# Routed rows that hold their last 64 features twice, so that one product turns two groups of 128 rows

## The reference

```
pooled = x.reshape(64, 12, 14, 16, 14, 16).sum(axis=(3, 5))
h = einsum('bcij,ce->bije', pooled, channel_weights).reshape(64, 196, 192)
h = h + attention(layernorm(h))        # 12 heads, weights relu(1 + qk + qk^2/2), normalised
flat = layernorm(h)                    # 12544 tokens of 192 features
top_w, top_i = top_k(softmax(flat @ router_w.T), 2)   # 2 of 8 experts
out = h + sum over the 2 experts of w_e * (gelu(flat @ w1[e] + b1[e]) @ w2[e] + b2[e])
```

## Time and profile before

| | us |
|---|---|
| median of 3 runs | 1308.08 (1303.27 to 1308.3) |
| profiled execution, its own time | 1309.67 |
| its span, first to last instruction | 1307.8 |
| TensorE busy | 1207.0 (92%) |
| VectorE busy | 883.9 (68%) |
| ScalarE busy | 593.6 (45%) |
| GpSimd busy | 559.2 (43%) |

### The profile page before, as it was taken

One profiled execution on the slowest core, in us unless ns is written; L12 is line 12 of the kernel. 1 busy time (PEld: TensorE's weight loads), 2 busy tenths in 40 slices (PEclk: granted clock), 3 DMA queues, 4 the chain that ended last, 5 costly groups with the idle time before them and its releaser, 6 DMA issues.

```text
span 1307.8 us, 25915 instructions
## 1 busy us (share of the span) xinstructions
PE 1207.0 (92%) x7219; PEld 1078.2 (82%) x7219; DVE 883.9 (68%) x2860; ACT 593.6 (45%) x1143; POOL 559.2 (43%) x453
## 2 busy tenths in 40 slices
PE   5867865999999999999999999999999899999996
PEld 3756754888889788989898989898989788899996
DVE  6788887686969686878778787878755332233443
ACT  0222223453545454545454545454545544545564
POOL 0103332315445445453636363635463654443533
PEclk9986556999999999999999999999999999999998
DMA  9789987778888788879798978798744655444555
GB/s 354 232 283 346 347 317 248 208 231 237 240 256 236 236 234 250 226 241 255 237 257 236 256 240 251 238 255 251 184 125 81 200 131 107 100 108 90 119 140 116
DMA packets 124823, 284.41 MB, mean 217 GB/s; under 512 B 23091, under 2 KB 68772, under 8 KB 124772
## 3 DMA queue, kind: packets, MB, share of 16 engines
q1 hardware_dynamic: 82570, 241.95, 55.8%
q0 software_dynamic: 41568, 41.24, 18.7%
q10 hardware_dynamic: 634, 0.61, 0.2%
HBM read 228.79 MB, written 54.95 MB: 217 GB/s over the span
## 4 chain that ended last, share of the span: by engine, by line
PE 68%; DVE 15%; issue 7%; ACT 4%; another core or an unknown queue 2%; DMA 2%; SPq 1%; ACTq 0%; DVEq 0%; POOLq 0%; POOL 0%
PE ps L1005 24%; PE ps L974 20%; PE ps L814 6%; PE ps L921 3%; PE ps L910 3%; DVE red L1086 2%; PE ps L945 2%; PE ps L946 2%; PE ps L888 2%; PE ps L900 2%; DVE red L1083 1%; PE ps L878 1%; DVE topi L1222 1%; DVE w1l L1342 1%
## 5 line engine op out<-in xcount | busy, mean ns | idle before, releaser
L631 POOL DMA_INDIRECT result<-ys,ridx x210 | 333.6, 1589 | 316.8 <-issue 195.4
L1005 PE MATMUL ps<-w2a,hid 128*128 x2520 | 460.7, 329 | 1.4 <-ACT hid L739 1.4
L1005 PEld LDWEIGHTS ps<-w2a,hid 128*128 128x128 f32 x2520 | 418.0, 191 | 14.6 <-issue 3.2
L616 POOL DMA_INDIRECT rows_d<-rows,sloti x224 | 217.0, 969 | 379.4 <-ACT rows L728 182.8
L739 ACT ACTIVATE hid<-ps,b1s 128x512 f32<-128x512 f32 (+1 forms) x344 | 223.0, 655 | 225.4 <-PE ps L974 172.6
L1086 DVE TENSOR_REDUCE red<-xbuf 128x21 f32<-128x672 f32 x344 | 279.0, 842 | 5.0 <-PE ps L878 2.5
L974 PE MATMUL ps<-xh,w1h 128*128 128x512 f32 (+1 forms) x344 | 165.2, 480 | 6.8 <-issue 5.0
L1342 DVE TENSOR_TENSOR w1l<-w1r,w1h 128x768 fp32r<-128x768 f32 x116 | 110.5, 953 | 82.2 <-ACT w1h L751 72.9
L974 PE MATMUL ps<-xh,w1l 128*128 128x512 f32 (+1 forms) x344 | 130.8, 380 | 0.0
L974 PE MATMUL ps<-xl,w1h 128*128 128x512 f32 (+1 forms) x344 | 130.8, 380 | 0.0
L974 PE MATMUL ps<-xb,w1h 128*128 128x512 f32 (+1 forms) x344 | 130.4, 379 | 0.0
(11 more groups left out here) (162 smaller groups left out, 1563.3 us busy)
## 6 DMA issues: line engine op xcount, KB each, us to landing
xbuf<-x SPq DMA_DIRECT2D x224, 672.0 KB
w1r<-L_ffn_w SPq DMA_DIRECT2D x118, 384.0 KB
xr<-rows_d SPq DMA_DIRECT2D x48, 402.0 KB
result<-h1s SPq DMA_DIRECT2D x16, 588.0 KB, 8.0
w2a<-L_ffn_w SPq DMA_DIRECT2D x8, 576.0 KB, 7.3
rows_d<-pad SPq DMA_DIRECT2D x9, 402.0 KB
rows_d<-rows,sloti POOLq DMA_INDIRECT x224
result<-ys,ridx POOLq DMA_INDIRECT x210
```

What stands on the lines that cost most here:

```text
L616: pool.indirect_dma_start(rows_d, bass.IndirectOffsetOnAxis(ap=sloti[:, k * RT + t:k * RT + t + 1], axis=0), rows[:, t, :], None).then_inc ...
L631: pool.indirect_dma_start(out, bass.IndirectOffsetOnAxis(ap=ridx[:, b, n:n + 1], axis=0), ys[:, b, n, :], None, compute_op=ALU.add).then_i ...
L1005: last = mm(yout(g, b, n), hid[:, m % 3, cols], w, start=False, stop=m == MC - 1 and n % 2 == 1)
```

## The change

Rows grow from 201 to 265 words. The new layout is: features 128 to 191, features 0 to 127, the gates, the number, and features 128 to 191 once more. A row's last 64 words and the first 64 words of the next group's row then lie side by side in `xr`, and one 128x128 product turns both: its result has the one group's features on partitions 0 to 63 and the next group's on 64 to 127. `X1` needs two products for a tile in place of four (one in place of two for a half tile). Even groups now have their high part in the upper half of `xb` and the low part in the lower half, odd groups the other way round, so ScalarE's copy and VectorE's subtraction become two instructions each on half as many columns. `V` writes each row tile with two ACTIVATEs of 128 columns, of which the second reads its 64 features twice. The scatters, the row loads and the padding move 1060 bytes a row in place of 804. `attA` shares memory with `gws`, `attB` with `us`.

```diff
 RES = E + NE
-ROW = E + NE + 1
+ID = E + NE
+ROW = ID + 1 + E - 128
...
-        gws = sb("gws", [NF, IPS, NV])
-        us = sb("us", [NF, HEADS, IPS, HV])
+        first_half = sb("products_or_turned_a", [KA, max(IPS * NV, NT * TOK)])
+        second_half = sb("weights_or_turned_b", [KB, max(IPS * NV, NT * TOK)])
+        gws = first_half[0:NF, 0:IPS * NV].rearrange("p (i v) -> p i v", i=IPS)
+        us = second_half[0:NF, 0:IPS * NV].rearrange("p (h i v) -> p h i v", h=HEADS, i=IPS)
+        attA, attB = first_half[:, 0:NT * TOK], second_half[:, 0:NT * TOK]
...
-        attA = sb("attA", [KA, NT * TOK])
-        attB = sb("attB", [KB, NT * TOK])
...
-        rows = sb("rows", [RP, RT, ROW])
+        rows_w = sb("rows", [RP, RT * ROW + ID + 1 - KB1])
+        rows = rows_w[:, 0:RT * ROW].rearrange("p (t c) -> p t c", t=RT)
...
+        def last_rows(t, half, nb, g, odd):
+            return t[half * KB1:(half + 1) * KB1, nb, 0:128 * g].rearrange(
+                "p (a o r) -> p a o r", o=2, r=128)[:, :, odd]
+
+        def turned_rows(b, odd, g):
+            return ps[odd * KB1:(odd + 1) * KB1, bank(b, "X1"), 0:64 * g].rearrange("p (a r) -> p a r", r=128)
...
                 for t in pair(q):
-                    last = nc.scalar.activation(rows[:, t, 0:E], h1s[:, t, 0:E], ACT.Identity,
-                                                bias=shift2[:, t:t + 1], scale=rstd2[:, t:t + 1])
+                    ends = rows_w[:, t * ROW:t * ROW + 2 * (ID + 1)].rearrange("p (a c) -> p a c", a=2)[:, :, 0:KB1]
+                    for o, i in ((rows[:, t, KB1:E], h1s[:, t, 0:128]),
+                                 (ends, h1s[:, t, 128:E].unsqueeze(1).to_broadcast([RP, 2, KB1]))):
+                        last = nc.scalar.activation(o, i, ACT.Identity, bias=shift2[:, t:t + 1],
+                                                    scale=rstd2[:, t:t + 1])
                 last.then_inc(s_norm, 1)
...
-                    copy(xb[KB1:128, nb, 0:128 * g], ps[KB1:128, bank(b, "X1"), 0:128 * g]).then_inc(s_xa, 1)
+                    for o in range(2):
+                        last = copy(last_rows(xb, o, nb, g, o), turned_rows(b, o, g))
+                    last.then_inc(s_xa, 1)
...
-                for n in range(groups(j + 1)):
-                    last = turn(ps[:, bank(b, f"X{q}"), n * 128:(n + 1) * 128], xr[:, nb, n, q * KB1:q * KB1 + 128])
+                if q == 0:
+                    for n in range(groups(j + 1)):
+                        last = turn(ps[:, bank(b, "X0"), n * 128:(n + 1) * 128], xr[:, nb, n, KB1:E])
+                else:
+                    for n in range(0, groups(j + 1), 2):
+                        both = xr[:, nb].rearrange("p n c -> p (n c)")[:, n * ROW + ID + 1:(n + 1) * ROW + KB1]
+                        last = turn(ps[:, bank(b, "X1"), n * 64:n * 64 + 128], both)
                 last.then_inc(s_xt, 1)
...
-                    V.tensor_tensor(xb[0:KB1, nb, 0:128 * g], ps[KB1:128, bank(b, "X1"), 0:128 * g],
-                                    xb[KB1:128, nb, 0:128 * g].bitcast(F32), ALU.subtract).then_inc(s_xd, 1)
+                    for o in range(2):
+                        last = V.tensor_tensor(last_rows(xb, 1 - o, nb, g, o), turned_rows(b, o, g),
+                                               last_rows(xb, o, nb, g, o).bitcast(F32), ALU.subtract)
+                    last.then_inc(s_xd, 1)
```

More of the change, by code:

```diff
@@ L604, in _ @@
             set_wait(pool, "pool", "zeros")
-            given("pool", "pad", nc.gpsimd.tensor_copy(pad[:, :, ROW - 1:ROW].bitcast(I32), padi[:].unsqueeze(2)))
+            given("pool", "pad", nc.gpsimd.tensor_copy(pad[:, :, ID:ID + 1].bitcast(I32), padi[:].unsqueeze(2)))
             def Q(s, q):
@@ L1248, in S11 @@
                     dve.wait_ge(d_scat, s * (32 * RT))
-                mark(V.tensor_copy(rows[:, :, ROW - 1:ROW].bitcast(I32), ids[:].unsqueeze(2)))
+                mark(V.tensor_copy(rows[:, :, ID:ID + 1].bitcast(I32), ids[:].unsqueeze(2)))
                 own(s)
@@ L1348, in I @@
                 g = groups(j + 1)
-                V.tensor_reduce(ridx[:, nb, 0:g], xr[:, nb, 0:g, ROW - 1:ROW].bitcast(I32), AX.X,
+                V.tensor_reduce(ridx[:, nb, 0:g], xr[:, nb, 0:g, ID:ID + 1].bitcast(I32), AX.X,
                                 ALU.max).then_inc(s_idx, 1)
```

## The result

| | before | after |
|---|---|---|
| median of 6 runs each, same chip | 1308.19 us (1303.27 to 1311.97) | 1328.62 us (1321.26 to 1332.34) |
| profiled execution: own time, span | 1309.67, 1307.8 | 1321.5, 1319.7 |
| TensorE, VectorE busy | 1207.0, 883.9 | 1192.1, 893.4 |
| ScalarE, GpSimd busy | 593.6, 559.2 | 637.1, 554.3 |
| bytes moved | 284.41 MB | 299.01 MB |

The ratio is 1.0143, with a 95% interval of 1.0103 to 1.0182: 1.4% slower. The profiled execution of after is one of its two shortest (the others took 1327 to 1332 us), so its trace shows some 12 us of the 20.

The account below looks back on a forecast made before the run. TensorE was taken to bound most of the run, with ScalarE's `V` delaying it at b = 2. Products -8.8, b = 2 +14.4, steps 0 to 3 +8.3, padding +3.4 gave +17.3 us: 1325 us, range 1310 to 1340.

Parts of the forecast that it names:

- `V` and its place, b = 2: Third tile of a step: six dearer row tiles ahead of `xh` make `M0` late by 1.2 us, 12 times: +14.4 us.
- The cover on VectorE: Tile with b = 2: VectorE is at earlier work for 0.90 us after `xh` ends, hiding that much of its delay.
- Rival A: Second ACTIVATE in the shadow of the first, 0.05 us a row tile: not slower, 1304 or 1301 us; 8%.
- The products: `X1` on TensorE: 106 products fewer, 0.22 us a tile and 0.11 a half tile, -8.8 us in sum.
- Steps 0 to 3: Before the three-tile steps: dearer `V` adds 1.9 us in each of three steps and 2.5 in step 3: +8.3 us.
- The padding: Behind step 15: eight padding blocks grow by 1.05 MB, so tile 38's rows come 3.4 us later (0 to 4.9).
- Nothing there: DMA in the steps: longer scatters and row loads cost nothing; GpSimd's idle time covers adds delayed by later landings.
- Rival C: TensorE's stop at `S3`, 10.8 us over the stage, absorbs the later arrival; the steps give 0, 1316 us; 20%.
- Rival B: TensorE's longer waits before `M4` and `M0` drop its clock once in each of 12 steps: +20 us, 1345; 12%.

Follow-up runs that it names:

- after_v_one: The changed kernel with one ACTIVATE of 192 columns a row tile in `V`, the last 64 words of a row left zero: 1316.6 us, ratio 1.0101 to the kernel before.
- after_both: The changed kernel with GpSimd's adds ahead of the scatters and `X0` (with `xh`) ahead of `V.1` and `V.2`: 1296.33 us, ratio 0.9919 to the kernel before.
- share_only: The kernel before with the shared tensors alone (`attA` in the memory of `gws`, `attB` in that of `us`): 1309.98 us, ratio 1.0002.
- v_two: The kernel before with `V` in two ACTIVATEs of 128 columns and the shared tensors, rows still 201 words: 1322.24 us, ratio 1.0135.
- adds_first: The kernel before with GpSimd's adds moved ahead of the scatters, each tensor in its own memory: 1286.61 us, ratio 0.9830.
- shared_adds_first: The kernel before with the shared tensors and GpSimd's adds ahead of the scatters: 1286.28 us, ratio 0.9828.
- after_adds_first: The changed kernel with GpSimd's adds ahead of the scatters: 1304.6 us, ratio 0.9978 to the kernel before.
- wide_adds_first: The kernel before with rows of 265 words, shared tensors and GpSimd's adds ahead of the scatters, old `V` and `X1`: 1292.41 us, ratio 0.9876.
- wide_rows: The kernel before with rows of 265 words (last 64 zero) and the shared tensors, old `V` and `X1`: 1322.31 us, ratio 1.0127.

## Why the prediction was right, and where it was wrong

**The total.** 1325 was predicted and 1328.6 measured, with the sign right. But the sum was made of parts, and two parts that it did not have, 20 us less at `S3` and 15 us more at b = 1, nearly cancelled. Nothing in the prediction says that they would: that the total came so close is luck.

**`V` and its place, b = 2: right.** Forecast +14.4, measured 200.2 - 185.4 = +14.8. An ACTIVATE of 128 columns takes 481 ns (forecast 484), and eight take 3.19 us, so they start (3.19 - 0.48) / 7 = 0.387 us apart: 0.77 a row tile in place of 0.444, +0.33. The cover on VectorE was 0.9 as read, and `M4` is late by 1.16. With one ACTIVATE put back (after_v_one) the twelve tiles take 188.1, so 12.1 us of the 14.8 are `V`'s, and the rest is the split copies and subtractions with the wider rows. With the copy moved ahead instead (after_both) they take 191.8, which shows the chain through `xh` by another cut. Rival A (the second ACTIVATE nearly free, 1304) fell by the first row of the profile.

**The products: right in kind, small in size.** Forecast 0.22 us a tile. The tiles of 22.57 and 22.40 us (shared and changed, adds first) differ by 0.17, those with b = 0 by 0.20, and the ten tiles to tile 48 give 2.0 of 2.2. The half tiles give nothing back: eight of them take 0.7 us more in place of 0.9 less. With the adds first one is seen waiting for its row load, which is the larger one:

```profile
1232.73 0.43 PE L831 MATMUL ps<-cst,xr 128*128 128x128 f32 x2 [1.12 <-DMA xr<-rows_d]
```

**Steps 0 to 3: too large.** Forecast +8.3; `S1` of step 4 starts 4.4 us later (with the adds first 6.0 later). The timelines say where: `V` of steps 1, 2 and 3 starts at 134.38, 174.01 and 211.09 in before and at 135.49, 176.50 and 212.99 in after. I had charged 1.9 for each of three steps. The first two took 1.8 and 1.4 (`V` of step 0 starts 0.7 earlier in after), the third gave 0.6 back, and the end of step 3 then took the forecast 2.5. Against share_only, where `S1` starts at 220.4, the changed kernel is 6.6 later and v_two, with `V` in two parts alone, 7.0: so it is `V`'s price, and nearer to the forecast. That the kernel before takes 2.2 us more than share_only up to there stays open. The end of the chain in step 2, which answers to the earlier trace rows:

```profile
135.49 5.48 ACT L743 ACTIVATE rows<-h1s,shift,roots 112x128 f32<-112x128 f32 x14
140.87 0.43 ACT L700 COPY gts<-ps 13x364 f32<-13x364 f32 x1
141.21 0.80 ACT L702 COPY phiT<-ps 91x784 f32<-91x784 f32 x1
...
152.71 0.31 DVE L1226 RECIPROCAL rden<-ps 98x24 f32<-98x24 f32 x1 [2.01 <-PE ps L938]
```

The 0.44 us before the second copy is used up, as forecast, and VectorE waits 2.01 in place of 0.24. `S1` of step 4 shows the end of step 3, as in the earlier trace rows: the wait for the last pooling has grown from 1.33 to 2.09.

```profile
227.01 2.06 PE L895 MATMUL ps<-mixg,red 128*98 128x96 f32 x12 [2.09 <-DVE red L1105]
```

**The padding: right in this trace, not shown as a price.** The wait answers to the earlier trace rows; the window behind it to the earlier trace rows.

```profile
1058.17 1.12 PE L831 MATMUL ps<-cst,xr 128*128 128x128 f32 x4 [6.51 <-DMA xr<-rows_d]
...
1048.00:1058.20 10.20, 3.69 (x20) 2.90 (x18) 0.31 (x2) 2.73 (x6) 5.56 (x5) 0.93 0.90 222
1058.20:1061.60 3.40, 3.40 (x12) 3.16 (x13) 0.98 (x3) 0.59 (x1) 2.79 (x3) 0.50 0.91 290
```

6.51 in place of 2.81 is +3.7, with +3.4 forecast. But over all kernels the same wait takes 2.81 (before), 3.36 (share_only), 3.13 (v_two), 6.12 and 6.38 us (adds_first, shared_adds_first) with rows of 201 words, and 5.53 to 8.26 with 265. TensorE arrives at another time in each, and that moves the wait as much as the bytes do. Between shared_adds_first and after_adds_first this stretch of two tiles costs nothing (45.1 and 44.3 us); in wide_adds_first it takes 46.8.

**The step that failed** is this one: "a later landing delays them, and GpSimd is busy only 361 of 754 us, so its idle time covers it". With it fell the "Nothing there" ahead of it: the wide rows cost 16 us against share_only, and 6 with the adds first. Most of GpSimd's idle time was not spare. It issues, waits for landings and issues again, and this chain goes round once in a step. I averaged it over steps 5 to 13 from the starts and ends in GpSimd's timelines (us); what ends each wait is told behind the table:

| | 14 scatters | of it, two waits for landing | wait behind adds 1 | behind adds 2 | before the next scatters | first scatter to first scatter |
|---|---|---|---|---|---|---|
| before | 24.2 | 3.6, 3.5 | 7.8 | 4.3 | 8.2 | 66.6 |
| share_only | 28.1 | 5.8, 5.2 | 6.5 | 5.0 | 5.6 | 66.8 |
| after | 27.5 | 5.5, 5.0 | 7.4 | 4.8 | 5.7 | 67.4 |
| wide_rows | 28.2 | 5.6, 5.2 | 7.5 | 5.1 | 5.9 | 68.5 |
| adds_first | 29.0 | 6.1, 5.3 | 7.0 | 6.3 | 0.3 | 65.0 |
| shared_adds_first | 28.7 | 5.7, 5.5 | 6.9 | 7.2 | 0.3 | 64.9 |
| wide_adds_first | 28.6 | 5.9, 5.5 | 8.0 | 6.7 | 0.3 | 65.7 |
| after_adds_first | 27.7 | 5.6, 4.7 | 7.6 | 8.4 | 0.3 | 65.8 |

Four adds take some 7.2 us to issue, three times in a step. For after: 27.5 + 3 x 7.2 + 7.4 + 4.8 + 5.7 = 67.0, which is the length of its step. GpSimd's busy time counts only the issues. Such a sum closes for every kernel, since it counts all of GpSimd's time; whether GpSimd bounds is told by what ends its waits. The traces of after and wide_rows have the landing of every add: in steps 5 to 13 the first scatter follows the landing of the last add by 1.2 us in 16 of 18 steps, and the adds follow landings by 1.0 to 1.1 us. So there GpSimd stands for its own transfers. In before it does not: in seven of the nine steps ScalarE's `V` ends the wait before the first scatter (7.0 to 9.3 us), and the chain of its page has no GpSimd. So the kernel before had some time to spare at this place (an estimate: its 8.2 us less the 5.6 of share_only are 2.6). In share_only the 20 us at `S3` (over the 11 tiles with b = 0) went, the two waits inside the scatters grew by 3.9 us together, and the spare time was used up.

With the adds ahead of the scatters the scatters need not wait for the adds' landing, and the last wait falls to 0.3. In after_adds_first and shared_adds_first eight of nine waits behind adds 2 end with `ys` of ScalarE, so GpSimd has time to spare and the step is as long as TensorE makes it; in wide_adds_first all nine end with a landing, and some of the waits at b = 1 are left. By the ratios the move took 22 us from the changed kernel and 22 from the one before, while GpSimd did the same work. That much is shown. In the changed kernel it takes away the waits at b = 1 (285.6 to 268.8 us in the traces). In the one before it takes away the stop at `S3` (315.5 to 295.7), and how it does that is not shown.

My first reading of the changed kernel's trace, that wider scatters land later (6.07 and 5.48 us where before had 3.38 and 2.69 at the same place), fell with share_only and is not kept: its waits for landing are as long with 201 words. What 265 words add is about 1 us behind the first adds (6.5 to 7.5; with the adds first 6.9 to 8.0 in wide_adds_first) and a few tenths elsewhere, 1.7 us a step together. Twelve such steps are 20 us; the ratios of share_only and wide_rows differ by 16 us. Why the wait lies there is argued only: those adds are queued behind the last scatters.

**Why the parts do not add.** TensorE's chain (with `V`) and GpSimd's run beside each other, and the longer one counts. In the trace of v_two tiles with b = 2 take 12.4 us more than in share_only and those with b = 1 take 10.7 less. Against share_only, `V` in two parts costs 17 us and the wide rows 16; with the products all three cost 18. The traces place the 18 (6.6 up to `S1` of step 4, 8.2 in the steps, 3.5 in the two tiles before tile 38), but of the 17 only 9, 7.0 of them up to `S1` of step 4: the rest lies in executions of v_two that have no trace. Without GpSimd's bound the whole change costs 1304.6 - 1286.3 = 18.3 us, beside a forecast of 17.3. So my sum held for a kernel in which GpSimd does not bound, and there the terms were b = 2 +14.9, products in the steps -4.2, everything up to tile 1 +7.5, tiles to 48 -2.8, half tiles +1.2: +16.6 by the starts of `M0` of tile 56.

**Rival C (absorbed, 1316): half seen.** The stop at `S3` did vanish, which I gave as the way to 1316, and it was even larger than the 10.8 us in the list of waits (315.5 - 295.7 = 20 us over 11 tiles). But share_only shows what that is worth: the same 20 us come back at b = 1 while GpSimd sets the length of the step. Since the stop vanishes with the shared tensors and also with the moved adds, it is not a price of either. What the engines waited for at `S3` in the kernel before stays open; no run was made for it. VectorE stands there as well: in the step at 640 us it is idle for 1.09, 0.55 and 0.34 us between small instructions of stage `L`, while TensorE is idle for 0.33 and 0.51.

**Rival B (the clock, 1345): not seen at `M4`.** The window from 696 to 700 us, behind the wait of 1.16 us, has the full clock; behind the wait of 3.03 us at b = 1 it fell for a while. The columns are as in the earlier trace rows.

```profile
696.00:700.00 4.00, 4.00 (x24) 3.77 (x24) 3.55 (x12) 2.31 (x4) 2.20 (x3) 1.00 0.64 160
...
670.00:673.40 3.40, 3.40 (x18) 3.12 (x17) 2.82 (x5) 1.36 (x3) 2.79 (x3) 0.65 0.69 187
673.40:676.80 3.40, 3.40 (x18) 3.16 (x17) 2.02 (x13) 1.18 (x2) 1.38 (x1) 0.84 1.10 298
```

The 0.65 and 0.84 are means over stretches partly at 1.2 GHz: 3.4 x (0.35 + 0.16) = 1.7 us lost after one such wait. In the steps of after the clock fell three times, behind waits at b = 1 of 3.08, 3.03 and 1.45 us, and not behind one of 2.59. In wide_rows four waits at b = 1 of 3.8 to 4.6 us were each followed by a longer stretch:

```profile
392.50:399.20 6.70, 6.60 (x22) 5.92 (x23) 4.48 (x13) 1.53 (x4) 4.64 (x3) 0.50 0.89 221
```

Four of these are some 4 x 6.7 x 0.5 = 13 us, most of which stands in its 304.2 us for b = 1. share_only has five stretches of 3.4 us at 0.50 in the steps, some 8 us. So the clock did cost time, though behind other waits than rival B named, and some 5 us of what the wide rows cost is the clock's. The Trainium skill ("TensorE: Matmul & The Clock Gate", under "HAM oscillation") tells of waits that return in each iteration and drop the clock each time. The waits of 1.2 us at `M4` returned in each of the twelve steps without a fall here; of the four longest waits at b = 1 (1.45 to 3.08 us) three had one.

## What to carry to other kernels

The busy share of an engine that issues transfers and waits for landings says nothing of its slack. Go through its waits round one step and see which end with a landing of its own and which with another engine's work: only the second kind hides a delay. In its order, put work that only needs issuing ahead of a long series, so that a wait for landing runs beside it; and before pricing a change, see whether a second chain is as long as the one being priced. An instruction on few columns is mostly fixed cost, so one split in two needs cover for a whole further instruction.

## What the runs showed of the hardware that was not expected

- A series of six indirect scatters of 112 rows took as long to land with 1060 bytes a row as with 804: waits of 5.6 and 5.2 us on the mean of nine steps in wide_rows, 5.8 and 5.2 in share_only.
- The same series at another moment of the step, in the kernel before, showed 3.6 and 3.5 us. Something other than the bytes moved the landing by 2 us, and a third more bytes did not; no run shows what it was.
- Adds by indirect DMA behind the scatters held GpSimd for 6.5 to 8.0 us on the mean from the last issue until the next adds could go, as long as the 7.2 us in which it issues four of them.
- A wait of TensorE costs more than its length when the granted clock falls behind it: 6.7 us at 0.50 behind waits of 3.8 to 4.6 us (wide_rows), while twelve waits of 1.15 us, one in each step, left the clock at 1.00 (after).
